# The second layernorm's halves by DMA transposes, and zero point and bias by one more matmul: a cross-attention and FFN kernel

## The reference

```python
x = x + xattn(_layernorm(x), ctx, Wq, Wk, Wv, Wskip)
x = x + ffn(_layernorm(x), qweight, scales, zeros, bias)
# xattn: energy = (Wq up)^T (Wk down) / sqrt(128); softmax; times (Wv down); plus Wskip up
# ffn:   w = (nibbles(qweight) - round(zeros/scales)) * scales;  y = x @ w + bias
```

## Time and profile before

| | us |
|---|---|
| median of 3 runs (616.62 to 617.56) | 616.7 |
| the profiled execution, its own time | 616.67 |
| its span | 614.8 |
| mean granted TensorE clock | 0.989 of full |

### The profile page before, as it was taken

How to read it: one execution, slowest core, us unless ns; L and a number is a source line. 1 busy time by engine, 2 the same in 40 slices (tenths; PEclk the granted TensorE clock), 3 DMA queues, 4 the chain that set the end, 5 groups by cost and what they waited for, 6 DMA issues and landing times.

```text
span 614.8 us, 10932 instructions
## 1 busy us (share of the span) xinstructions
PE 588.1 (96%) x3348; PEld 416.1 (68%) x3348; DVE 476.5 (77%) x1027; ACT 409.4 (67%) x976; POOL 468.7 (76%) x520
## 2 busy tenths in 40 slices
PE   2868999999999999999999999999999999999996
PEld 2755777667777766777776677777677777667763
DVE  6787877878887777888778788878777877887762
ACT  4874677666668766666876666686666677666650
POOL 2453788777879877777977787897778789777866
PEclk9977999999999999999999999999999999999999
DMA  8011012222111222211222211122221112221002
GB/s 315 3 43 43 27 53 79 77 77 73 40 53 66 77 77 77 70 41 47 73 77 77 77 65 46 43 77 77 77 77 54 57 43 77 77 77 68 19 19 102
DMA packets 20178, 41.38 MB, mean 67 GB/s; under 512 B 2496, under 2 KB 7104, under 8 KB 20160
## 3 DMA queue, kind: packets, MB, share of 16 engines
q1 hardware_dynamic: 19584, 41.03, 19.7%
q10 hardware_dynamic: 576, 0.14, 0.1%
HBM read 24.39 MB, written 16.78 MB: 67 GB/s over the span
## 4 chain that ended last, share of the span: by engine, by line
PE 91%; DVE 5%; ACT 2%; issue 1%; DMA 1%; POOLq 0%; POOL 0%; ACTq 0%
PE ps_y L676 36%; PE ps_e L610 17%; PE ps_o L644 14%; PE ps_t L625 9%; PE ps_o L637 7%; PE ps_t L657 5%; PE ps_kv L688 2%; PE ps_kv L686 2%; DMA sb_x<-in_x_dram 1%; DVE sb_nib L457 1%; ACT sb_prob L288 1%; DVE sb_pt_lo L408 1%; DVE sb_neg_max L398 0%; ACT sb_pt_hi L297 0%; DVE sb_zp L499 0%
## 5 line engine op out<-in xcount | busy, mean ns | idle before, releaser
L288 ACT ACTIVATE sb_prob<-ps_e,sb_neg_max 128x256 f32<-128x256 f32 x256 | 118.7, 470 | 128.9 <-DVE sb_neg_max L398 128.8
L676 PE MATMUL ps_y<-sb_wf,sb_xnt_hi 128*128 128x512 f16 x512 | 196.1, 383 | 0.9 <-DVE sb_xnt_lo L448 0.9
L676 PE MATMUL ps_y<-sb_wf,sb_xnt_lo 128*128 128x512 f16 x512 | 194.0, 379 | 0.0
L214 POOL TENSOR_SCALAR sb_prob<-sb_prob,sb_rsum 128x256 f32<-128x256 f32 x256 | 117.7, 477 | 27.5 <-DVE sb_rsum L403 27.5
L408 DVE TENSOR_TENSOR sb_pt_lo<-ps_t,sb_pt_hi 128x512 fp32r<-128x512 f32 x128 | 88.3, 691 | 34.6 <-ACT sb_pt_hi L297 30.4
L398 DVE TENSOR_REDUCE sb_neg_max<-ps_e 128x2 f32<-128x512 f32 x128 | 87.7, 686 | 34.8 <-PE ps_e L610 34.8
L610 PE MATMUL ps_e<-sb_kv_hi,sb_xc_hi 128*128 128x256 f32 x256 | 91.6, 358 | 7.7 <-DVE sb_kv_lo L535 4.0
L297 ACT ACTIVATE sb_pt_hi<-ps_t 128x512 fp32r<-128x512 f32 x128 | 76.3, 598 | 33.9 <-PE ps_t L625 33.9
L676 PEld LDWEIGHTS ps_y<-sb_wf,sb_xnt_hi 128*128 128x128 f16 x512 | 49.7, 97 | 59.2 <-issue 17.6
L223 POOL TENSOR_TENSOR sb_rstd<-sb_ve,sb_neg_half 128x1 f32<-128x1 f32 x32 | 17.5, 548 | 92.3 <-DVE sb_ve L443 92.3
L250 POOL TENSOR_TENSOR sb_xc_lo<-sb_xc,sb_xc_hi 128x1024 fp32r<-128x1024 f32 x32 | 76.5, 2390 | 9.2 <-ACT sb_xc_hi L343 7.5
(11 more groups left out here) (85 smaller groups left out, 1162.9 us busy)
## 6 DMA issues: line engine op xcount, KB each, us to landing
sb_x<-in_x_dram SPq DMA_DIRECT2D x32, 512.0 KB, 3.3
out_dram<-sb_o SPq DMA_DIRECT2D x64, 256.0 KB, 2.1
sb_ctx<-in_ctx_dram SPq DMA_DIRECT2D x32, 128.0 KB, 2.5
sb_q<-in_L_ffn_qweight_dram SPq DMA_DIRECT2D x4, 512.0 KB, 6.4
sb_scale_row<-in_L_ffn_scales_dram SPq DMA_DIRECT2D x1, 512.0 KB, 8.7
sb_bias_row<-in_L_ffn_bias_dram SPq DMA_DIRECT2D x1, 512.0 KB, 9.5
sb_wk<-in_L_xattn_Wk_dram SPq DMA_DIRECT2D x1, 64.0 KB, 3.4
sb_wq<-in_L_xattn_Wq_dram SPq DMA_DIRECT2D x1, 64.0 KB, 3.3
```

What stands on the lines that cost most here:

```text
L214: last = pool.tensor_scalar(prob[:, j, t, :], prob[:, j, t, :], rsum[:, j, t:t + 1], 1.0, ALU.mult, ALU.mult)
L288: done = act.activation(prob[:, j, t, :], ps_e[j % 2][:, t, :], ACT.Exp, bias=neg_max[:, j, t:t + 1], accum_out=esum[:, j, t:t + 1])
L676: last = pe.matmul(ps_y[h][:, :], xnt_p[s][:, kt, :], wf[:, kt, h * HALF:(h + 1) * HALF], start=kt == 0 and s == 0, stop=kt == KT - 1 and ...
```

## The change

The normalised row is split into float16 halves before it is transposed (`split_xn` on ScalarE, `split_xn_lo` on VectorE, both in SBUF), and SP transposes both halves by DMA into double-buffered `xnt_hi` and `xnt_lo`. TensorE's `transpose_xn` goes. The zero-point term and the bias come in by one more matmul a half: `seed_l` holds the row sum's high, low and high part and ones in rows 0, 1, 32, 64 and 96, `seed_row` the zero-point row's parts and bias divided by scale. GpSimd splits the row sum, three small DMAs carry it from a column to rows of `seed_l`. `x1` has three buffers, and GpSimd adds it alone. SP, ScalarE and VectorE have all steps written out in place of the loop. The core of the diff:

```diff
 # SP, step(b, par), between the stores and the loads; p = b - 1
+                if ran(p):
+                    sp.wait_ge(xnhi_done, p + 1)
+                    if ran(p, 2):
+                        sp.wait_ge(y_done[1], p - 1)
+                    sp.dma_start_transpose(xnt_hi[:, 1 - par, :, :], xn_hi[:, :, :].rearrange(
+                        "c k r -> c (k r)")).then_inc(xnt_loaded[1 - par], 16)
+                    sp.wait_ge(xnlo_done, p + 1)
+                    sp.dma_start_transpose(xnt_lo[:, 1 - par, :, :], xn_lo[:, :, :].rearrange(
+                        "c k r -> c (k r)")).then_inc(xnt_loaded[1 - par], 16)
...
+                    for k, row in ((0, 0), (1, 1), (0, 32)):
+                        sp.dma_start(seed_l[row:row + 1, 1 - par, :].bitcast(F32),
+                                     rs3[:, 1 - par, k:k + 1].bitcast(F32)).then_inc(rs_loaded[1 - par], 16)
 # ScalarE
+            def split_xn(p, par):
+                act.wait_ge(xn_done, p + 1)
+                if ran(p, 1):
+                    act.wait_ge(xnt_loaded[1 - par], arrived(p - 1, 1 - par, 32))
+                act.activation(xn_hi[:, :, :].rearrange("c (t e) r -> c t e r", e=2),
+                               xn[:, :].rearrange("c (t r e) -> c t e r", e=2, r=P),
+                               ACT.Copy).then_inc(xnhi_done, 1)
 # VectorE, behind probs_lo(b, 1)
+            def split_xn_lo(p, par):
+                dve.wait_ge(xnhi_done, p + 1)
+                if ran(p, 1):
+                    dve.wait_ge(xnt_loaded[1 - par], arrived(p - 1, 1 - par, 32))
+                dve.tensor_tensor(xn_lo[...], xn[...], xn_hi[...], ALU.subtract).then_inc(xnlo_done, 1)
 # TensorE
-                if ran(p):
-                    transpose_xn(b, p, 0)
                 if ran(b):
                     skip(b, par, 1)
-                if ran(p):
-                    transpose_xn(b, p, 1)
 # ffn
                     if h == 0:
-                        pe.wait_ge(xntlo_done[0], c + 1)
+                        pe.wait_ge(xnt_loaded[cpar], arrived(c, cpar, 32))
...
                 if g == 3:
-                    last.then_inc(y_done[h], 1)
+                    if h == 0:
+                        pe.wait_ge(rs_loaded[cpar], arrived(c, cpar, 48))
+                    pe.matmul(ps_y[h][:, :], seed_l[:, cpar, :], seed_row[:, h * HALF:(h + 1) * HALF],
+                              start=False, stop=True).then_inc(y_done[h], 1)
```

More of the change, by code:

```diff
@@ L90, in xattn_ffn_program @@
         pt_hi, pt_lo = (sb(n, [P, HALVES, MT, HALF], F32R) for n in ("pt_hi", "pt_lo"))
[L91 removed]
+        x1 = sb("x1", [P, 3, N])
         xn = sb("xn", [P, N])
[L93 to L95 removed]
+        xn_hi, xn_lo = (sb(n, [P, KT, P], F16) for n in ("xn_hi", "xn_lo"))
+        xnt_hi, xnt_lo = (sb(n, [P, 2, KT, P], F16) for n in ("xnt_hi", "xnt_lo"))
+        seed_row = sb("seed_row", [P, OUT], F32R)
+        seed_l = sb("seed_l", [P, 2, P], F32R)
+        seed_tmp = sb("seed_tmp", [P, OUT])
+        rs3 = sb("rs3", [P, 2, 2], F32R)
         prod = sb("prod", [P, HALVES, HALF])
@@ L182, in step @@
                     sp.dma_start(x_sb[:, par, :], x[b + 2, :, :]).then_inc(x_loaded[par], 16)
-            run_steps(sp, step)
+            for b in range(-1, B + 3):
+                step(b, b % 2)
             for par in range(2):
@@ L196, in _ @@
             pool.wait_ge(ident_made, 2)
+            pool.memset(seed_l[:, :, :].bitcast(F32), 0.0).then_inc(seed_made, 1)
+            pool.wait_ge(seed_made, 1)
+            for k in (2, 3):
+                pool.memset(seed_l[32 * k:32 * k + 1, :, :].bitcast(F32), 1.0).then_inc(seed_made, 1)
+            pool.wait_ge(seed_made, 3)
             def write_out(q, par, h):
@@ L201, in write_out @@
                 if h == 0:
-                    pool.wait_ge(rest_done, q + 1)
+                    pool.wait_ge(x1_done[1], q + 1)
                     if ran(q, 2):
@@ L239, in step @@
                 if ran(p):
[L241 to L247, removed]
+                    split_row_sum(p, 1 - par)
                 if ran(n):
@@ L329, in step @@
                     probs_hi(b, 1)
+                if ran(p):
+                    split_xn(p, 1 - par)
                 if isinstance(b, int) and b in (0, 1):
@@ L370, in step @@
                     unpack(2 * b + 1)
-            run_steps(act, step)
+            for b in range(-1, B + 3):
+                step(b, b % 2)
         @block.vector
@@ L573, in step @@
                     probs_lo(b, 1)
+                if ran(p):
+                    split_xn_lo(p, 1 - par)
                 if isinstance(b, int) and b == 1:
@@ L578, in step @@
                     scale_product(q, 1)
-            run_steps(dve, step)
+            for b in range(-1, B + 3):
+                step(b, b % 2)
         @block.tensor
```

128 lines of the change are left out of this document (61 added, 67 removed).

## The result

The changed kernel took 626.69 us (median of 4 runs, 626.18 to 627.26) against 616.66 us before: ratio 1.0163, 95% interval 1.0144 to 1.0182. It is slower by 1.6%, as forecast and within the range, but by 10 us where the forecast had 35. What came is rival 1, transposes in time, whose figure was 629.

The account below looks back on a forecast made before the run. TensorE, busy 96% of the span, was taken as the bound before, with the DMA transposes deciding the step after. 616.67 plus 19 (steps), 12 (start) and 4 (end) gave 651.7 us, range 620 to 710.

Parts of the forecast that it names:

- rival 1: Middle steps: DMA transposes arrive in time, the pair under 5.9 us; step 17.94, total 629 us; chance 0.31.
- The DMA transposes: Ahead of each step's FFN: two transposes of 3.3 us, one after the other, 6.6; step 18.64, +0.63.
- The sum's +19: Middle steps: waiting for the transposes adds 0.63 us a step over 30 steps, +19 us.
- point of decision (5.9): Transposes ahead of the FFN: a pair of up to 5.9 us costs nothing, each further us costs 30.
- the wait at L700: FFN's first matmul waits for the second transpose, step 18.6; nil or over 1.6 us would prove the forecast wrong.
- 8.7: Upper bound in us for one DMA transpose, taken from the slowest 512 KB load, a row repeated over partitions.
- The loop through ScalarE and VectorE: Middle steps: VectorE's queue takes back nearly all TensorE gave, 17.94 against 18.01, -0.07 a step, if transposes are in time.
- The start: At b = 1: eight more VectorE operations, 13.9 us, less 2 for TensorE's transposes; +12 (6 to 13).
- The end: Last FFN: nothing covers the transposes, +3.5, and 0.5 for the last extra matmuls; +4 taken.
- GpSimd's 138 us: GpSimd in each step: loses two additions of 2.4 us, gains two one-column operations; not waited for, worth nothing.
- The loops written out: Loops of SP, ScalarE and VectorE: writing them out changes nothing, since rows already follow without a gap.
- Rival 3: Middle steps: TensorE stays the bound, `split_xn_lo` under 0.83 us, step 17.55; 609.7 (chance 0.05) or 616, no change (0.04).

Follow-up runs that it names:

- experiment 8: Changed kernel with VectorE's two products moved from ahead of `probs_lo(2)` and `residual(0)` to behind the first half's statistics: 609.31 us, ratio 0.9886.
- experiment 10: Kernel of experiment 6 with the transposes back on TensorE and their PSUM copies on ScalarE and VectorE, extra matmul kept: 616.4 us, ratio 1.0008.
- experiment 1: Changed kernel with the seed's eight operations at the start cut to two casts, output not exact: 617.5 us, ratio 1.0012.
- experiment 6: Changed kernel with the seed's rows computed small, as 128x8, then laid out as rows by five 4 KB DMAs: 612.29 us, ratio 0.9944.
- experiment 4: Kernel before the change with only the loops of SP, ScalarE and VectorE written out: 616.2 us, ratio 0.9997.
- experiment 5: Changed kernel with the split right behind `xn`, ahead of `probs_hi(0)` on ScalarE and `probs_lo(0)` on VectorE: 628.03 us, ratio 1.0186.
- experiment 3: Changed kernel with only the high half transposed by DMA, the FFN multiplying by the high half twice: 623.5 us, ratio 1.0118.

## Why the prediction was right and wrong

- **The step that failed** is in "The DMA transposes": "I take 3.3 each, ... and one after the other, since both go through one queue: 6.6". The 3.3 was right. The second half was not: two transfers of one queue were under way together, 1.31 us apart, and the pair took about 4.5. The sum's +19 therefore never came; the steady part was -5.4. By the prediction's own point of decision (5.9) this is rival 1, and so by its signs: in the middle steps the wait at L700 is nil and `skip(b, 1)` waits for `x1`. In-order issue was taken for in-order execution. The earlier trace rows alone could not have told it, but SP's timeline of the kernel before beside them could:

```profile
312.39 1.57 SPq L175 DMA_DIRECT2D out_dram<-sb_o  x2
```

These are two stores of 256 KB on the same queue, issued at 312.39 and 313.60. The first lands 2.1 after its issue, at 314.5. The second was issued 0.9 ahead of that, and lands 2.1 after its own issue all the same; as two transfers one after the other it would have taken 3.0.

- **A bound was misread.** 8.7 was taken as the slowest 512 KB load; the page of before has one of 9.5 (the row of the bias). The choice of 3.3 and the sum do not hang on it.
- **The rule of the Trainium skill** (Advanced Engine Details and Errata, X-Bar Transpose: as fast as regular DMAs) would have made each 2.1. The trace differs: 3.2 to 3.3 for 256 KB where the stores of 256 KB take 2.0. But the conclusion drawn from it, 629, was nearer than mine. The figure of the Trainium skill (VectorE: DVE Perf Modes, The three transpose paths: 1309 ns for a block), if multiplied by eight, is an estimate of 10.5 us, far from the 3.3 measured.
- **The loop through ScalarE and VectorE was right** to 0.1 us at each station. Offsets from the scores' start, predicted and measured: second transposes done 8.33, 8.34; `split_xn` starts 8.87, 8.86; `split_xn_lo` done 11.28, 11.27; products done 12.5, 12.47; `probs_lo(2)` done 13.1, 13.07; `attend` done 16.2, 16.09; the step 17.94, 17.83. That VectorE takes back what TensorE gives was the forecast's second half, and experiment 8 shows it: without the products in the way the step is 17.25. One reason in it was wrong, and its number right by luck: TensorE's waits at the scores (0.33, and 0.03 of issue, which turn 8.46 + 0.23 into 8.33) were to go because ScalarE and VectorE leave the transposed row alone. Experiment 10 keeps that work and loses the waits too; what it lacks is GpSimd's addition beside VectorE's row.
- **The start** was priced 13.9 for the eight operations, measured 13.2 (reciprocal 6.1 forecast, 6.55 measured; all four casts at the low end, 0.69), and +12 for TensorE, measured 12.2. Experiments 1 and 6 show that it is as large as the whole loss.
- **The end** was priced +4 in the forecast, with 0.5 for the last matmuls in it, and +2 in rival 1; measured 2.4 and 0.5. The 0.4 us for which SP still holds a store ahead of the first transpose was in no term.
- **GpSimd's 138 us** were priced at nothing, since it was not waited for. Its own work was not, but it held up VectorE: 0.23 a step in experiment 10's comparison, an estimate of 7 us over 30 steps. `split_xn_lo` was not held by GpSimd (1.24 in the middle). The copies of `rs3` were not waited for, landing 2.1 after their issue.
- **The loops written out** cost nothing, as priced (experiment 4).
- **The missed version.** Rival 3 put the way to the gain in `split_xn_lo` taking under 0.83 us. The way that worked was to take the two products out of its shadow; the prediction had listed them among the stations, at 1.21 us, but had not asked whether they must stand there.

Two things stay open, since they were not tried: whether part of the reciprocal's 6.55 us was a wait for GpSimd's operation of 2.35 us beside it (five traces have both, with GpSimd 0.2 to 0.6 behind, and the reciprocal took 6.55 in each), and places for the split other than the two of the changed kernel and of experiment 5.

## What to carry to other kernels

Work taken off the busiest engine is worth only what the second-longest loop leaves: walk that loop station by station, and move whatever in it is not needed there (here two products, worth 0.58 us a step) before judging the change. Price the one-off operations of a start by their free size, and lay small vectors over the partitions before computing on them: 13.2 us became one. For transfers of one queue, look in the trace for whether they overlap before adding their times.

## What the runs showed of the hardware that was not expected

- Two DMA transposes of 256 KB on one queue overlap: issued 1.31 us apart (each issue holds SP 1.26 to 1.32 us), each landing 3.2 to 3.3 us after its issue began. The queue's packets rose from 19,584 to 100,992 and its share of the DMA engines' time from 20% to 34%, with no effect on the loads of x (3.3 as before). With one transpose a step (experiment 3) it has 67,200 packets, so 32 transposes make 33,792 of them, 1,056 each.
- A reciprocal on 64 partitions of 1024 columns took 6.55 us, 6.4 ns a column, where a multiplication of the same size (L541) took 1.22.
- A cast of 1024 columns that takes 0.69 us by itself took 2.72 beside a GpSimd operation with two SBUF inputs (experiment 1): its one SBUF input was enough. The other way round, GpSimd's four normalisations took 2.80 instead of 1.84 (experiment 5). And a VectorE operation of 128 columns (L531) took 0.58 beside GpSimd's addition instead of 0.35 (experiment 10).
- After the same wait of 3.1 us TensorE ran the last FFN's first 16 matmuls in 3.63 us in some traces (granted clock 1.00 in that of the changed kernel) and in 5.31 in others (0.67 to 0.68; experiments 1, 5 and 8): 1.7 us between two executions that no edit explains.
- A column of 128 single elements copied into a row takes 2.1 us to land, about as long as a 256 KB store (2.0).
